# A fused AdaLN, Mamba and FFN block in fp32: engine steps rearranged, the FFN bias spread by transposes, a fourth product tile, 26 products per round on GpSimd

## The reference

```python
mod = (silu(c) @ wmod).reshape(2, 6, 1, 512)
sa, ca, ga, sb, cb, gb = (mod[:, i] for i in range(6))
ga = (2 * (ga >= 0) - 1) * maximum(abs(ga), 0.25)      # gb the same
h = layernorm(x) * (1 + ca) + sa
x = x + ga * mamba(h)
h = layernorm(x) * (1 + cb) + sb
x = x + gb * (einsum('btd,rde->bte', h, factors) / sqrt(8) + bias)
```

## Time and profile before

| | us |
|---|---|
| median of 3 runs | 2000.46 (1999.31 to 2001.25) |
| the profiled execution, its own time | 2002.29 |
| its span in the trace | 2000.6 |
| busy: PE, PEld | 1794.8 (90%), 1337.8 (67%) |
| busy: DVE | 1811.3 (91%) |
| busy: ACT | 1548.5 (77%) |
| busy: POOL | 1825.4 (91%) |

### The profile page before, as it was taken

How to read it: one execution, slowest core, us unless ns; L and a number is a source line. 1 busy time by engine, 2 the same in 40 slices (tenths; PEclk the granted TensorE clock), 3 DMA queues, 4 the chain that set the end, 5 groups by cost and what they waited for, 6 DMA issues and landing times. The chain is left out here.

```text
span 2000.6 us, 29195 instructions
## 1 busy us (share of the span) xinstructions
PE 1794.8 (90%) x9096; PEld 1337.8 (67%) x9096; DVE 1811.3 (91%) x2232; ACT 1548.5 (77%) x4501; POOL 1825.4 (91%) x756
## 2 busy tenths in 40 slices
PE   7967988999899898999999899899989999899798
PEld 4656757677585766767576675767757576676664
DVE  3898989989899998989989898999999999898995
ACT  3858778787887878788786887878788787878762
POOL 1899999999999999999999999999999999999992
PEclk9997989989999998999999898998999999899898
DMA  5656404031230403214032240403223040311300
GB/s 179 247 116 176 130 22 158 23 142 59 80 116 28 158 22 127 75 56 135 33 133 89 81 141 22 158 23 137 64 80 117 27 158 22 119 57 44 105 27 32
DMA packets 72000, 186.17 MB, mean 93 GB/s; under 512 B 6818, under 2 KB 8482, under 8 KB 63908
## 3 DMA queue, kind: packets, MB, share of 16 engines
q1 hardware_dynamic: 68148, 176.95, 25.7%
q0 software_dynamic: 3696, 7.34, 2.3%
HBM read 172.20 MB, written 12.06 MB: 92 GB/s over the span
## 5 line engine op out<-in xcount | busy, mean ns | idle before, releaser
L605 POOL TENSOR_TENSOR ub<-u,b_all 128x2048 f32<-128x2048 f32 x255 | 1167.7, 4579 | 40.3 <-DMA b_all<-bc_scratch 40.3
L759 ACT ACTIVATE decay<-dt,decay_rate 128x256 f32<-128x256 f32 x2048 | 882.3, 465 | 22.4 <-DVE state_p L1522 3.4
L1522 DVE TENSOR_TENSOR_SCAN decay<-decay,ub 128x512 f32<-128x512 f32 x589 | 700.8, 1215 | 32.2 <-ACT decay L759 30.9
L623 POOL TENSOR_TENSOR state_p<-state_p,c_all 128x1024 f32<-128x1024 f32 (+1 forms) x256 | 531.2, 2075 | 92.8 <-ACT carry L745 54.3
L1522 DVE TENSOR_TENSOR_SCAN state_p<-decay,ub 128x512 f32<-128x512 f32 x435 | 512.2, 1209 | 41.1 <-ACT decay L759 40.7
L1093 PE MATMUL y_bank<-ident,sc_d 128*128 128x128 f32 x2356 | 353.5, 282 | 144.0 <-DVE sc_d L1537 143.8
L1093 PEld LDWEIGHTS y_bank<-ident,sc_d 128*128 128x128 f32 x2356 | 277.3, 144 | 233.9 <-DVE sc_d L1537 174.8
L1537 DVE TENSOR_TENSOR sc_d<-decay,c_all 128x512 f32<-128x512 f32 x589 | 380.8, 678 | 42.3 <-PE y_bank L1093 34.7
L745 ACT ACTIVATE carry<-decay 128x2 f32<-128x2 f32 x589 | 96.1, 163 | 270.9 <-DVE sc_d L1537 270.0
L1093 PEld LDWEIGHTS y_bank<-ident,state_p 128*128 128x128 f32 x1740 | 217.2, 149 | 69.0 <-issue 37.6
L1093 PE MATMUL y_bank<-ident,state_p 128*128 128x128 f32 x1740 | 240.7, 286 | 15.1 <-POOL state_p L623 15.0
(11 more groups left out here) (137 smaller groups left out, 1876.7 us busy)
## 6 DMA issues: line engine op xcount, KB each, us to landing
win_h<-win_m SPq DMA_DIRECT2D x128, 256.0 KB, 2.6
win_z<-win_m SPq DMA_DIRECT2D x128, 256.0 KB, 3.0
b_all<-bc_scratch SPq DMA_DIRECT2D x31, 1024.0 KB, 4.7
c_all<-bc_scratch SPq DMA_DIRECT2D x31, 1024.0 KB, 5.2
xa<-x SPq DMA_DIRECT2D x16, 512.0 KB, 5.1
xc<-x SPq DMA_DIRECT2D x16, 512.0 KB, 3.7
out<-xc SPq DMA_DIRECT2D x15, 512.0 KB, 3.8
ffn<-factors POOLq DMA_DIRECT2D x7, 1024.0 KB, 10.4
```

What stands on the lines that cost most here:

```text
L605: pool.tensor_tensor(ub[:, slot, :, :, :], u[:, (PAIRS * c + q) % U_PAIRS, :, :].unsqueeze(1).to_broadcast([P, QUAD, 2, ROWS]), b_all[:, n ...
L623: pool.tensor_tensor(part, part, c_all[:, n:n + k, :].unsqueeze(2).to_broadcast([P, k, 2, ROWS]), ALU.mult).then_inc(pooled, 1)
L759: last = act.activation(bk[:, j * ROWS:(j + 1) * ROWS], dt[:, pair % DT_PAIRS, j, :], ACT.Exp, scale=decay_rate[:, e, n:n + 1])
L1522: dve.tensor_tensor_scan(dst, bk[:, :], ub[:, quad % UB_RING, i, :, :].rearrange("p j r -> p (j r)"), 0.0, ALU.mult, ALU.add).then_inc(sca ...
```

## The change

`D_RING` goes from 3 to 4. `EVERY_POOL` has 26 ones and twos in place of 28, so two more units of each of rounds 2 to 15 are multiplied on DVE; they are in quads 2 and 14 (units 10 and 58, steps 5 and 29), and one unit of quad 6 changes places with one of quad 7. The bias comes in as 128 x 4 columns with one DMA; PE turns the gate into columns (`turn_gate`, step 16 of round 0), `scale_bias` works on 128 x 8 elements, one operand in PSUM, and `spread_bias` opens a bank with four transposes of a broadcast column in place of the matmul of `bias_row`. SP's two DMAs of line 506 go, and so does ACT's wait for `bias_scaled` ahead of one softplus; SP's first load of `xc` and PE at step 26 of round 0 wait for `bias_scaled` instead. The rest moves pieces between steps; of those that the diff below leaves out, the last quarter of `project_dt` goes from step 19 to 18.

```diff
-D_RING = 3
+D_RING = 4
-M_AT = (2, 1)
-IN_AT = ((2, 3, 4, 5, 7, 8, 9, 10), (2, 3, 4, 5, 8, 9, 10, 11))
+M_AT = (2, 2)
+IN_AT = ((2, 3, 4, 5, 7, 8, 9, 10), (1, 3, 4, 5, 8, 9, 10, 11))
-EVERY_POOL = (2, 2, 2, 1) * PAIRS
+EVERY_POOL = (2, 2, 1, 1, 2, 2, 1, 2, 2, 2, 2, 1, 2, 2, 1, 1)
...
             sp.dma_start(ffn[:, :, :], fac_v[0]).then_inc(ffn_loaded, 16)
-            for b in range(BATCH):
-                sp.dma_start(bias_row[b:b + 1, :], bias.rearrange("(a d) -> a d", a=1)).then_inc(bias_loaded, 16)
+            sp.dma_start(bias_in[:, :], bias).then_inc(bias_loaded, 16)
...
-                        for b in range(BATCH):
-                            sp.dma_start(bias_gate[b:b + 1, :], gb[0:1, b, :]).then_inc(bias_gated, 16)
...
-                    if lc is not None and s == 23:
+                    if lc is not None and s == 24:
                         modulate_after(c - 1, 1)
-                        if s == 19:
+                        if s == 20:
                             skip(c + 1, 0)
-                        if s in (27, 31) and (c + 1) % PER:
+                        if s in (26, 31) and (c + 1) % PER:
                             seam_decays(c + 1, s // 31)
-                        if s == 21:
+                        if s == 22:
                             z_after(c - 1)
-                        if s == 22:
+                        if s == 23:
                             modulate_after(c - 1, 0)
...
+            def spread_bias(t, b):
+                for k in range(KD):
+                    pe.matmul(bank_c[t][:, k * P:(k + 1) * P], bias_col[:, k, b:b + 1].to_broadcast([P, P]), ident[:, :],
+                              start=(k == 0), stop=False, is_transpose=True, skip_group_check=True)
+            def turn_gate():
+                pe.wait_ge(rows_made, 2 * BATCH)
+                for k in range(KD):
+                    for b in range(BATCH):
+                        at = k * BATCH + b
+                        last = pe.matmul(bank_c[0][:, at:at + 1], gb[0:BATCH, b, k * P:(k + 1) * P], ident[0:BATCH, 0:1],
+                                         start=True, stop=True)
+                last.then_inc(gate_turned, 1)
...
-                pick = ident[0:BATCH, c // PER:c // PER + 1].to_broadcast([BATCH, P])
-                pe.matmul(bank_c[t][:, :], pick, bias_row[:, :], start=True, stop=False)
+                spread_bias(t, c // PER)
...
-                        if s in (22, 23, 26, 27):
-                            expand_dt(c + 1, s - 22 - 2 * (s // 26))
+                        if s == 21:
+                            expand_dt(c + 1, 0)
+                        if s == 22:
+                            expand_dt(c + 1, 1)
+                        if s == 26:
+                            expand_dt(c + 1, 2)
+                        if s == 27:
+                            expand_dt(c + 1, 3)
...
+                        for q, at in enumerate((13, 15, 15, 15)):
+                            if s == at:
+                                project_out(c - 1, 1, q)
...
                         if s == 23:
                             ffn_bias(c - 1, 0)
                             project_ffn(c - 1, 0, (0,))
-                        if s == 24:
+                        if s == 23:
                             project_ffn(c - 1, 0, (1, 2, 3))
...
             def scale_bias():
-                dve.wait_ge(bias_loaded, 16 * BATCH)
-                dve.wait_ge(bias_gated, 16 * BATCH)
-                dve.scalar_tensor_tensor(out=bias_row[:, :], in0=bias_row[:, :], scalar=math.sqrt(RANK), in1=bias_gate,
+                dve.wait_ge(bias_loaded, 16)
+                dve.wait_ge(gate_turned, 1)
+                dve.scalar_tensor_tensor(out=bias_col[:, :, :], in0=bank_c[0][:, 0:KD * BATCH].rearrange("p (k b) -> p k b", b=BATCH),
+                                         scalar=math.sqrt(RANK), in1=bias_in[:, :].unsqueeze(2).to_broadcast([P, KD, BATCH]),
                                          op0=ALU.mult, op1=ALU.mult).then_inc(bias_scaled, 1)
...
-                    if c + 2 < CHUNKS and s == 28:
+                    if c + 2 < CHUNKS and s == 29:
                         shifts(c + 2, mv_a, nrm_a, norm_a)
-                    if lc is not None and s == 20:
+                    if lc is not None and s == 21:
                         shifts(c - 1, mv_c, nrm_c, norm_c)
-                        if s == 6:
-                            gate_sums(c - 1, 0)
-                        if 6 <= s <= 8:
-                            gate_sums(c - 1, s - 5)
+                        for q, at in enumerate((6, 6, 7, 10)):
+                            if s == at:
+                                gate_sums(c - 1, q)
-                        if s == 27:
+                        if s == 28:
                             add_ffn(c - 1, 0)
```

More of the change, by code:

```diff
@@ L231, in build @@
         small = sb("small", [P, 3, LB])
-        bias_row = sb("bias_row", [BATCH, DIM])
+        bias_in = sb("bias_in", [P, KD])
+        bias_col = sb("bias_col", [P, KD, BATCH])
         xa = sb("xa", [P, LB, DIM])
@@ L276, in build @@
         ga, gb = y_rows[:, :, DIM:2 * DIM], xc[:, :, :]
-        bias_gate = dt[0:BATCH, DT_PAIRS - 1, :, :].rearrange("p j r -> p (j r)")
         cond_all = xc[:, :, :].rearrange("p t d -> p (t d)").rearrange("p (k b q) -> p k b q", k=KD, b=BATCH)
@@ L310, in build @@
         wo_scaled, ffn_scaled = sem("wo_scaled"), sem("ffn_scaled")
-        wo_kept, wo_stored, ffn_kept, bias_gated = sem("wo_kept"), sem("wo_stored"), sem("ffn_kept"), sem("bias_gated")
+        wo_kept, wo_stored, ffn_kept, gate_turned = sem("wo_kept"), sem("wo_stored"), sem("ffn_kept"), sem("gate_turned")
         xc_loaded, bn_c, stats_c, norm_c, z_c = sem("xc_loaded"), sem("bn_c"), sem("stats_c"), sem("norm_c"), sem("z_c")
@@ L460, in load_xc @@
                     sp.wait_ge(ffn_scaled, HALVES)
+                    sp.wait_ge(bias_scaled, 1)
                 wait(sp, out_stored, 16 * c)
@@ L876, in soft_dt @@
                 act.wait_ge(a_full[q % 2], A_JOBS[q % 2] * c + 5 + q // 2)
-                if pair == DT_PAIRS - 1:
-                    act.wait_ge(bias_scaled, 1)
                 wait_u(act, pair - DT_PAIRS + 1)
@@ L994, in one_round @@
                     decays(2 * step)
-                    if 2 * s % N == 4 and pair:
+                    if s % 8 == 2 and pair:
                         copy_y(pair - 1)
@@ L1022, in one_round @@
                         make_column(c, 2)
+                    if c % PER and s == 12:
                         make_column(c, 3)
@@ L1277, in project_ffn @@
                     last = pe.matmul(bank_c[t][:, :], hT[c % H_RING][:, k, t * P:(t + 1) * P], ffn[:, k, :],
-                                     start=False, stop=(k == KD - 1))
+                                     start=False, stop=(k == KD - 1), skip_group_check=True)
                 if k == KD - 1:
@@ L1416, in one_round @@
                             mod_rows(4 + s // 9, 1)
+                        if s == 16:
+                            turn_gate()
                         if s == 26:
-                            pe.wait_ge(rows_made, 2 * BATCH)
+                            pe.wait_ge(bias_scaled, 1)
                     if la is not None:
@@ L1426, in one_round @@
                             project_h(c + 1, i // 2, i % 2)
[L1427 to L1430, removed]
+                        if s == 16:
+                            project_dt(c + 1, 0)
+                        if s == 18:
+                            project_dt(c + 1, 2)
+                        if s == 18:
+                            project_dt(c + 1, 3)
+                        if s == 18:
+                            project_b_c(c + 1, 0)
+                        if s == 19:
+                            project_b_c(c + 1, 1)
                         if s == 20:
                             project_b_c(c + 1, 2)
+                        if s == 20:
                             project_b_c(c + 1, 3)
-                        if s in (22, 23, 26, 27):
-                            expand_dt(c + 1, s - 22 - 2 * (s // 26))
+                        if s == 21:
[6 more added lines that the diff above has]
+                            expand_dt(c + 1, 3)
                     if lc is not None:
@@ L1438, in one_round @@
                             project_gate(c - 1, 2 + s // 2, s % 2)
-                        if 4 <= s <= 7:
-                            turn_sums(c - 1, s - 4)
+                        if s in (4, 5, 6, 7):
+                            turn_sums(c - 1, {4: 0, 5: 1, 6: 2, 7: 3}[s])
                     if lc is not None:
[L1442 to L1447, removed]
+                        for q, at in enumerate((9, 10, 11, 12)):
+                            if s == at:
+                                project_out(c - 1, 0, q)
+                        for q, at in enumerate((13, 15, 15, 15)):
+                            if s == at:
```

(6 more changed lines are left out.)

1 line of the change is left out of this document (removed).

## The result

The changed kernel takes 1932.9 us against 2000.9 of the kernel before in the same comparison: ratio 0.9657, 95% interval 0.9638 to 0.9676. The forecast was 1977 with a range of 1955 to 2000. The direction was right, the size was not: 68 us came where 24 were forecast. The profiled execution took 1932.15 us, its span is 1930.4. (One of its four runs was disturbed, 6163 us, and stands outside the ratio.)

A forecast was written before the change was run, and what follows sets the result against it. It held that the order of work inside a round, followed through VectorE, costs as much as the work. Terms -13 - 15 + 9 - 1.5 - 1.3 - 1.5 = -23.3 from 2002.3, less 1.8, gave 1977 us, range 1955 to 2000.

The forecast's parts named there:

- more goes: Rival: similar stalls at steps 2, 5, 22 and 25 also shrink, some 1.5 us a round, -20 us; 1957 us, chance 0.19.
- GpSimd's 2.03 us bring nothing by themselves, since VectorE never waited for it: Two products a round leave GpSimd: its saved time was booked as no gain, only as keeping it from becoming the bound.
- the stall at step 26: VectorE's product waits 2.30 us for its tile of the ring of three, in 11 of the 13 rounds.
- What VectorE pays: Two products added at steps 5 and 29: the first free, the second charged 0.68 us a round, +9 us in all.
- Fourth tile and FFN: Ring of four and earlier FFN work let the product waiting 2.30 us start at once: -1.2 us in 11 rounds, -13.
- Step 29: ScalarE's late exponentials: moving seam_decays, an add_ffn and shifts recovers 1.15 of a 1.45 us stall in 13 rounds, -15 us.
- The second norm: Shift, normalization and modulation one step later: booked at 0, bounds -0.81 (stall of step 22 goes) and +1.1 us a round.
- `scale_bias`: Round 0: 9.81 us become under 1, but GpSimd bounds rounds 0 and 1, so only -1.5 us booked, at most 1.7.
- The slower rival: FFN block in one piece between steps 23 and 24, at PE's lower clock, delays copy_y: 2026 us, chance 0.13.
- The end: Behind the last round, bias by transposes -1.3 us; in the last round, a 2.88 us stall at step 23 mostly goes, -1.5.

## Why the prediction was right or wrong

The steady round, from the runs: 118.9 before; 115.9 with the steps; 114.4 with steps and 26 products; bias and ring then add nothing. The forecast was 117.4, so 3.0 us a round were missed: 2.2 in the products and 0.8 in the moved steps. The rival "more goes" (1957) was nearest, and it too left the products as a cost. Of its four places two went in round 5 (steps 5 and 22), and two rose, from 0.61 to 0.75 us at step 2 and from 0.94 to 1.34 at step 25.

- **"GpSimd's 2.03 us bring nothing by themselves, since VectorE never waited for it" is the step that failed.** The term was +0.68 us a round where the runs show -1.5 (28 against 26 products in the new order). Rows 2 were read rightly for the old order: there PE's list of waits in rounds 2 to 14 has none for GpSimd, GpSimd is idle 6 us a round, and the same edit costs 0.55 us, near the +0.68. What failed was to carry that over to the new order. Once the stall at step 26 is gone, GpSimd's work up to the end of a round decides when PE closes the pair, when ScalarE's copy of y can go, and so when VectorE's scan at step 2 gets its exponentials; a list of VectorE's waits names only ScalarE. The run with quad 14's product put back shows it: +1.05 us at step 2 and +1.05 us a round. The prediction compared GpSimd's busy time (112.7, then 110.7) with the whole round and took the rest for reserve. With 28 products in the new order GpSimd was still idle 3.3 us a round, and it was late all the same, because it stood still early: in round 5 0.19, 2.11 and 0.50 us up to 754.91, and not once from there to the copy of the next step 2.
- **What VectorE pays** was nearly right. It was charged one product of 0.68 us. Its busy time rose by 10 us in 13 rounds from 28 to 26 products (1430.8 to 1440.8), 0.8 us for both together.
- **Fourth tile and FFN.** The stall of 2.30 us did go, and the term (-1.0 a round) was about right for the FFN block (1.1 by itself in the new kernel), but the tile had no part in it in the new kernel: three do as well. Whether it would have removed the stall by itself in the old order wasn't run. The bias, booked inside this term, is enough by itself to remove it (1.6 us a round alone), and so are the steps.
- **Step 29** was foreseen with its mechanism and nearly its size: 1.15 forecast, 0.8 measured, wait 1.44 without the moves.
- **The second norm** was booked at 0 with a bound of -0.81; it is worth 1.2 us a round, outside the bound. It clears the waits of steps 22 and 23 (0.81 and 0.37).
- **`scale_bias`**: booking its 9.81 us in full would have been wrong, and the 1.5 us booked were of the right kind. Round 1, cut by VectorE's scans, is 3.3 us shorter, over the bound argued, but GpSimd, whose list there is unchanged, is hardly further. It begins the same instruction at 313.48 us before and at 313.54 after:

```profile
313.48 4.54 POOL L605 TENSOR_TENSOR ub<-u,b_all 128x2048 f32<-128x2048 f32 x1
313.54 4.56 POOL L603 TENSOR_TENSOR ub<-u,b_all 128x2048 f32<-128x2048 f32 x1
```

  VectorE begins round 2 at 312.15 before and 309.39 after, so 2.8 of the 3.3 us are only VectorE coming closer to GpSimd. Counted from the start of round 0, GpSimd gains 0.6 us, and 1.2 with the bias alone. This fits GpSimd as the bound of these rounds. And the shorter round 1 doesn't need the new `scale_bias`: the steps alone, which keep the old one, give 120.3. By the Trainium skill, "SBUF — State Buffer", on the shared port pair, a VectorE instruction with two SBUF inputs and a GpSimd instruction that reads SBUF exclude each other. The 9.81 us fit: while the old instruction lasted, GpSimd ran instructions of 4.99, 1.74 and 2.81 us, so VectorE was kept out for longer than one of them. That one operand in PSUM is what brought it to 0.16 isn't shown, since the new instruction also has 8 elements per partition instead of 512.
- **The slower rival** didn't come. The rule of the Trainium skill, "TensorE: Matmul & The Clock Gate", Part 4, that transposes don't count for the clock, stood behind it. Its condition, the FFN block in one piece, saves 1.1 us a round in the new kernel. The bias alone puts transposes in place of matmuls, and the granted clock of rounds 2 to 14 goes from 0.95 to 0.97, not down. With the steps it is 1.00. Both changes also shift real matmuls or shorten PE's list, so the rule itself isn't refuted.
- **The end.** The last round and what follows gave 8.4 us, forecast 2.8. Alone, the bias gives 3.5 there (1.3 forecast), the steps 3.2 and the 26 products 0.9. The last FFN takes 7.13 us instead of 8.99, at a granted clock of 1.00 instead of 0.78; why the clock held there wasn't tested.

## What to carry to other kernels

An engine that the bottleneck never waits for can still make it late through two others: follow each wait back to what its releaser waited for, up to an engine that didn't wait, and do so again for the order that a change will make, since the first stall mended can bring the next engine into the chain. When two engines balance, ask of each piece of work not how long it is but whether its engine still stands still before somebody needs the result: the product with no such idle time behind it was worth three times the other, of equal length. And edits that look like separate gains may remove the same stall, or lose alone and win together; add them one by one and take them out one by one.

## What was not expected of the hardware

Two products added to VectorE raised its busy time by 0.8 us a round where their durations sum to 1.36 (28 to 26 on GpSimd). The next two raised it by 1.41 (26 to 24). Instructions that don't wait for each other overlap a little in these traces (a product from 759.75 for 0.67 us, the next scan from 760.33), and with the same 28 products VectorE was busy 1440.4 us in the old order and 1430.8 in the new, which has fewer stalls. So busy time isn't a sum of rows. Why the second two got nothing off isn't shown.
